# Order of the transfers in an attention stage: a stack load between the two halves of a table write, stores and value loads moved into odd heads

## The reference

```python
scores = jnp.einsum('bhqd,bhkd->bhqk', q, k) / scale
c2p = jnp.einsum('bhqd,hpd->bhqp', q, pos_k)            # 128 positions
c2p = jnp.take_along_axis(c2p, c2p_idx, axis=-1) / scale  # position q - k
p2c = jnp.einsum('bhkd,hpd->bhkp', k, pos_q)
p2c = jnp.swapaxes(jnp.take_along_axis(p2c, p2c_idx, axis=-1), -1, -2) / scale
probs = softmax(scores + c2p + p2c)
ctx = jnp.einsum('bhqk,bhkd->bhqd', probs, v)
```

## Time and profile before

| | |
|---|---|
| median of 3 runs | 5222.62 us (5219.48 to 5224.54) |
| the profiled execution, its own time | 5222.77 us |
| its span | 5220.9 us |
| PE busy / DVE / ACT / POOL | 4618.7 / 3524.1 / 2584.8 / 1925.2 us |
| DMA moved | 1461.31 MB, mean 280 GB/s |
| queue q1 (SP), share of 16 engines | 81.7% |

### The profile page before, as it was taken

How to read it: one execution, slowest core, us unless ns; L and a number is a source line. 1 busy time by engine, 2 the same in 40 slices (tenths; PEclk the granted TensorE clock), 3 DMA queues, 4 the chain that set the end, 5 groups by cost and what they waited for, 6 DMA issues and landing times. The chain is left out here.

```text
span 5220.9 us, 110891 instructions
## 1 busy us (share of the span) xinstructions
PE 4618.7 (88%) x31272; PEld 3293.2 (63%) x31272; DVE 3524.1 (67%) x9058; ACT 2584.8 (50%) x4809; POOL 1925.2 (37%) x4461
## 2 busy tenths in 40 slices
PE   6999999499999999999999999999999996771698
PEld 4666666276666666666666666666666664661565
DVE  3333333388888878888878878888888885775511
ACT  1222222266666666666666666666666661110011
POOL 1222222144444444444444444444444443550022
PEclk9999999799999999999999999999999997885599
DMA  4766767699999999999999999999999995771033
GB/s 137 237 225 223 235 223 231 212 349 353 351 340 348 343 331 351 346 336 347 343 328 344 353 332 342 345 337 346 339 342 344 350 340 168 250 241 61 9 90 73
DMA packets 672172, 1461.31 MB, mean 280 GB/s; under 512 B 48195, under 2 KB 290291, under 8 KB 671603
## 3 DMA queue, kind: packets, MB, share of 16 engines
q1 hardware_dynamic: 665462, 1446.22, 81.7%
q0 software_dynamic: 6144, 8.52, 1.0%
HBM read 738.61 MB, written 715.94 MB: 279 GB/s over the span
## 5 line engine op out<-in xcount | busy, mean ns | idle before, releaser
L1010 DVE CUSTOM_DVE_ANT_1 a_scored<-a_ps_m_s,a_bias 128x512 f32<-128x512 f32 x2048 | 1397.5, 682 | 575.2 <-PE a_ps_m_s L878 543.5
L947 ACT ACTIVATE a_probsT<-a_ps_m_t 128x512 f32<-128x512 f32 x2048 | 1227.1, 605 | 938.3 <-PE a_ps_m_t L887 936.3
L887 PE MATMUL a_ps_m_t<-a_ident,a_scored 128*128 128x128 f32 x8192 | 1264.5, 277 | 0.5 <-ACT a_probsT L947 0.5
L941 ACT ACTIVATE a_skew_in<-a_ps_m_tab 128x512 f32<-128x512 f32 x2048 | 1125.7, 614 | 199.7 <-DMA d_skew<-a_skew_in 140.5
L887 PEld LDWEIGHTS a_ps_m_t<-a_ident,a_scored 128*128 128x128 f32 x8192 | 938.9, 141 | 437.3 <-DVE a_scored L1017 352.1
L1017 DVE TENSOR_SCALAR a_scored<-a_scored,a_top_of 128x512 f32<-128x512 f32 x2048 | 1045.2, 530 | 0.0
L827 POOL TENSOR_SCALAR_AFFINE_SELECT a_bias<-a_bias 128x128 f32<-128x128 f32 (+2 forms) x2560 | 980.5, 410 | 71.9 <-POOL a_bias L827 63.1
L818 POOL COPY a_bias<-a_high 128x128 f32<-128x128 f32 (+1 forms) x1024 | 355.9, 376 | 1764.9 <-DMA a_bias<-d_skew 1763.6
L878 PE MATMUL a_ps_m_s<-a_ident,a_bias 128*128 128x128 f32 x5120 | 902.6, 273 | 0.0
L859 PE MATMUL a_ps_m_tab<-a_tabs,a_stack 96*128 96x256 bf16 (+1 forms) x4096 | 714.2, 276 | 192.5 <-ACT a_skew_in L941 122.2
L878 PEld LDWEIGHTS a_ps_m_s<-a_ident,a_bias 128*128 128x128 f32 x5120 | 683.4, 142 | 109.0 <-issue 3.1
(11 more groups left out here) (182 smaller groups left out, 3641.8 us busy)
## 6 DMA issues: line engine op xcount, KB each, us to landing
d_skew<-a_skew_in SPq DMA_DIRECT2D x1024, 480.0 KB, 7.7
a_bias<-d_skew SPq DMA_DIRECT2D x512, 896.0 KB, 8.9
a_stack<-d_stack SPq DMA_DIRECT2D x256, 384.0 KB
p_xt<-in_xT SPq DMA_DIRECT2D x32, 2048.0 KB, 9.2
d_ctx<-a_ctx_sb SPq DMA_DIRECT2D x128, 256.0 KB, 7.7
d_stack<-p_part_q SPq DMA_DIRECT2D x64, 384.0 KB, 2.8
d_stack<-p_part_k SPq DMA_DIRECT2D x64, 384.0 KB, 3.4
d_v<-p_v_sb SPq DMA_DIRECT2D x32, 544.0 KB, 3.0
```

The lines of the kernel that those rows point to most:

```text
L887: mm = pe.transpose(m_t[:, k % 2, t * P:(t + 1) * P], scored[:, hh % SCORED, t, k * P:(k + 1) * P], ident[:])
L941: nc.scalar.activation(skew_in[:, u, w, 2 * half:2 * half + 2], m_tab[:, w], ACT.Identity).then_inc(tab_kept, 1)
L947: nc.scalar.activation(turned_at(hh // GH, hh % GH, k), m_t[:, k % 2], ACT.Exp, scale=SCALE).then_inc(turned, 1)
L1010: nc.vector.tensor_tensor_reduce(split(scored[:, hh % SCORED, t]), split(m_s[:, t % 2]), extra, 1.0, -3.0e38, ALU.add, ALU.max, top_of[:, ...
```

## The change

`write_tables` is split into `write_half`, which issues one half of the write, and a version of itself for the first heads, before the loop. In the loop SP now issues the first half as soon as the tables are kept, then (even heads) the stack load and the key terms, then whatever values and context store the head has, then the second half. The value loads move from hh = 6 and 14 to 7 and 15, the context stores from hh = 2, 6, 10, 14 to 3, 7, 11, 15. Their waits ask for the same counts as before.

```diff
-            def write_tables(n, hh, par):
+            def write_half(par, p0):
 
                 u, slot = par % 2, par % RING
+                half, used = P // 2, QT * TW - P // 2
+                x0 = half - p0
+                sp.dma_start(bass.AP(scratch, slot * P * PITCH + p0 * (PITCH + 1) + x0,
+                                     [[PITCH + 1, half], [ROW, 2], [1, used]]),
+                             skew_in[p0:p0 + half, u].rearrange("p w t x -> p w (t x)")[:, :, x0:x0 + used]
+                             ).then_inc(skew_out[u], 16)
+
+            def write_tables(n, par):
+
                 settled(sp, tab_kept, 4 * (n + 1), passed)
-                half, used = P // 2, QT * TW - P // 2
-                for p0, x0 in ((0, half), (half, 0)):
-                    sp.dma_start(bass.AP(scratch, slot * P * PITCH + p0 * (PITCH + 1) + x0,
-                                         [[PITCH + 1, half], [ROW, 2], [1, used]]),
-                                 skew_in[p0:p0 + half, u].rearrange("p w t x -> p w (t x)")[:, :, x0:x0 + used]
-                                 ).then_inc(skew_out[u], 16)
+                write_half(par, 0)
+                write_half(par, P // 2)
...
                         read_tables(n + NEXT, b + m // NH, m % NH)
+                    writes = not (last and hh + LEAD >= NH)
+                    if writes:
+                        settled(sp, tab_kept, 4 * (n + LEAD + 1), passed)
+                        write_half(hh + LEAD, 0)
+
                     if hh % SH == 0:
                         g = hh // SH + SR - 1
                         if not (last and g >= NS):
                             settled(sp, s_done, QT * n, passed)
                             load_stack(b + g // NS, g % NS)
-                    if not (last and hh + LEAD >= NH):
-                        write_tables(n + LEAD, (hh + LEAD) % NH, hh + LEAD)
-
-                    if hh == TURN + GH and not early(b, hh, NH):
+                    if hh == TURN + GH + 1 and not early(b, hh, NH):
                         settled(sp, pv_done, n - hh, passed)
                         load_values(b, 1)
-                    if hh == NH // 2 + TURN + GH and not last:
-                        settled(sp, pv_done, n - TURN - GH, passed)
+                    if hh == NH // 2 + TURN + GH + 1 and not last:
+                        settled(sp, pv_done, n - TURN - GH - 1, passed)
                         load_values(b + 1, 0)
-                    if hh % GH == (KEPT + 1) % GH and not early(b, hh, KEPT):
+                    if hh % GH == (KEPT + 2) % GH and not early(b, hh, KEPT):
                         store_ctx(b, (hh - KEPT) // GH)
+                    if writes:
+                        write_half(hh + LEAD, P // 2)
```

More of the change, by code:

```diff
@@ L763, in _ @@
             for m in range(LEAD):
-                write_tables(m, m, m)
+                write_tables(m, m)
                 if m >= LEAD - NEXT:
```

## The result

The change made the kernel slower: 5328.2 us (median; 5317.9 to 5341.0) against 5221.1 us beside it, ratio 1.0211 with a 95% interval of 1.0183 to 1.0239. The prediction had said 5158, with 0.16 for slower, and its range ended at 5232. The interval lies above 1; whether the loss is over 2% it leaves open.

The account below looks back on a forecast made before the run. PE was taken to set the pace in most heads, the DMA queue in the others. Position and SP's time cost 0 and rate gained 65 us, so 5222.8 - 65 = 5158 us, range 5100 to 5232.

Parts of the forecast that it names:

- What bounds the kernel: Attention stage: PE sets the pace in most heads, the DMA queue, through late table writes, takes more in the others.
- Position in the queue: SP's issue order: the same transfers stand between second halves two heads apart as before; cost 0, gain 0.
- SP's time: Second half issued some 1.2 us later in even heads, hidden by the queue: cost 0; without that cover 307 us.
- 4.9 us of queue: Part of a half write's 7.7 us landing put down to transfers queued before it; taken to hide SP's later issue.
- Rival B: Even heads, ACT's wait before L941: second half lands 1.2 us later, up to 307 us, 5530 us; chance 0.11.
- Rate: Stack load moved from behind the read to between half writes: DMA engines faster, 65 us gained, half of 131.
- The windows after stack loads: Sign: eight 4 us windows after a stack load's issue rise from 320 to 340 GB/s or more; still 320 means wrong.
- A: DMA in the whole stage: only the bytes count, so order is neutral, 5223 us give or take 10; chance 0.17.
- C: Separated half writes: a half alone is slow, 384 pairs lose 1.4 us each, +538 us, 5760 us; chance 0.02.
- The port rule: Half writes: 64 partitions reach eight of sixteen ports, so a half alone runs at half of 435 GB/s, 2.3 us.
- D: Context store, ACT's wait at L953: lands too late, +38 us if it slips; chance 0.03 that it outweighs the gain.

Follow-up runs that it names:

- between2: Kernel before, with stack load and key terms moved between the two halves only in heads with hh % 4 = 2: 5340.5 us, ratio 1.0238.
- between0: Kernel before, with stack load and key terms moved between the two halves only in heads with hh % 4 = 0: 5210.3 us, ratio 0.9984.
- s_after_wait: Kernel before, with stack load and key terms issued behind the wait for the tables but ahead of both halves, which stay together: 5296.5 us, ratio 1.0158.
- s_between: Kernel before, with only stack loads and key terms moved between the halves, values and context stores left in place: 5331.7 us, ratio 1.0218.
- vc_between: Kernel before, with only values and context stores moved between the halves of odd heads, stack load ahead of the wait: 5251.8 us, ratio 1.0068.
- s_first_odd: Kernel before, with the stack load issued first in odd heads, before SP waits for the landing that the read needs: 5289.8 us, ratio 1.0129.
- s_first_even: Kernel before, with the stack load issued ahead of the read in even heads: 5196.4 us, ratio 0.9981.
- kt_ahead: Changed kernel, but with the key terms issued with the read, ahead of the wait for the tables: 5279.9 us, ratio 1.0123 to the kernel before.
- kt_between: Kernel before, with only the key terms moved between the halves, stack load ahead of the wait: 5217.3 us, ratio 1.0002.

## Why the prediction was wrong

**What bounds the kernel**: right. The same chain of waits that was read before grew with the time: in the 3050 us of the earlier trace rows ACT's wait grew by 72 us and PE's by 68, where the whole grew by 107.

**Position in the queue**: that the same transfers stand between second halves is true and was no protection. It holds a landing in place only as long as each transfer enters the queue in time: in heads with hh % 4 = 3 and 0 the second halves landed 0.5 and 0.7 us later after the tables than before.

**SP's time, costed at 0: this step failed.** The working named the cover (the load is issued while SP waits for the tables) and the price without it (1.2 us x 256 = 307 us), and then let "4.9 us of queue" hide it. That figure was the median landing of 1024 half writes less the landing of a lone transfer. It lumps four kinds of head together, and a landing is the end of the whole DMA, which doesn't tell how full the 16 engines are meanwhile. In heads with hh % 4 = 2 the cover was needed: with the load behind the wait there alone the kernel lost 2.4% (`between2`), as much as by the whole change. The delay was undersized as well. The second half of an even head was to go out 1.2 us later; it went out 2.5 us later where hh % 4 = 2 and 1.6 us later where it is 0. Rival B had the right place in SP's program and the right sign, with 0.11; but its mechanism, a late landing in every even head, is not what the runs show: where hh % 4 = 2 the second half lands 0.2 us earlier than before, and the late ones are in the two heads after it. The loss hangs on one kind of head alone, where it is 124 us / 128 = 1.0 us a head.

**Rate, 65 us of gain: mis-sized in time.** Its cleanest test is `between0`, the same order where it costs nothing. Of the 65 us half of the loads should have brought some 33; measured were 8, from 0 to 16 (0.16%, 0.01 to 0.30%). The windows after stack loads have a mean of 336 GB/s in the changed kernel against 320 for the earlier trace rows, but in single windows they lie between 245 and 400, and taken over the whole stage (220 and 228 of them) the means are 316 and 321. First and second of the eight, and the fifth:

```profile
2513.40:2517.40 4.00, 3.66 (x32) 2.55 (x32) 3.57 (x12) 3.34 (x7) 1.65 (x6) 1.00 1.03 376
2526.80:2530.80 4.00, 4.00 (x35) 2.71 (x34) 4.00 (x11) 2.46 (x6) 1.89 (x6) 1.00 1.02 400
...
2567.80:2571.80 4.00, 3.93 (x33) 3.13 (x30) 3.25 (x9) 3.71 (x8) 2.03 (x7) 1.00 0.86 245
```

So the windows after a stack load, from which the term was taken, did not get faster over the stage. The packets say more. In the trace's packet records, assigned to DMAs by their order, a packet of a stack load took 121 ns on average before and 101 ns after; with 192 packets a load and 256 loads on 16 engines that is about 63 us of the engines' time (an estimate from these figures), close to the 65 us of the term. But one of a table write went from 162 to 171 ns, 256 of them a head, which takes more than that back, and why is not shown. In `between0` the packets of q1 took 81.3% of 5216.9 us, 4241 us, 24 less than before; there some 20 us of new idle time (the span is only 4 us shorter) took most of that. So the faster stack load was real, and it didn't become time.

**The other rivals.** A (bytes alone) is refuted, the order matters by up to 2.4%. C (a half alone is slow, +538 us) is refuted: 128 pairs kept apart in `between0` cost nothing. The port rule of the Trainium skill (SBUF — State Buffer, "Door 1"), on which C rested, shows no effect in that run; whether it has a part in the 0.6% between `s_after_wait` and `s_between` is open. D (the store) did not come: L962 waited 3.9 us once, as before.

**Open**: whether the engines running short or SP's lateness in the next head passes the loss on; why the packets of the table writes took longer; what the values and stores cost by themselves (0.7% in `vc_between`, nothing on top of the stack loads); how moving 12 KB gives back 0.9%; and why `s_first_odd` lost 1.3%.

## What to carry to other kernels

When a DMA is moved in an in-order issue program, look at the time in which the issuing engine only waits: a transfer issued there takes none of the engine's working time, and the same transfer behind the wait can cost time though the order of the queue is unchanged (1.6% in `s_after_wait`). It is no rule that any transfer in such a place helps: `s_first_even` gained 0.2%, `s_first_odd` lost 1.3%. Look also at the head after the one that is changed, for the lateness shows there. Read the depth of the queue head by head, not from a median landing; a share of 1.00 over 1000 us says that it sufficed, not that there was some to spare. And before a cover is let go at no cost, test the cheapest run first: the same order with the transfer only moved past the wait.

## What the runs showed of the hardware

How long a DMA's issue on SP takes goes with its place in the sequence, not with its size (medians). Directly behind a read the stack load's issue takes 1.38 us and the key terms' behind it 0.29 us; behind a half write the load takes 0.39 us and the 12 KB behind it 1.41 us, up to 2.5 us. In `kt_ahead` the 12 KB stand directly behind the read and take 1.24 us, in `kt_between` directly behind a half write and take 0.38 us.

The size of the neighbour's effect on packets: a stack load's packet took 121 ns behind a read and 101 ns between two half writes.
